# Fused attention: the value matmuls of both query halves of a key tile issued together, behind the third score pair of the next tile

## The chip, the cores and the metric

One core of a Trainium2 chip runs the whole program in one launch. The metric is device time in microseconds (us), as the median of several executions. All stretches, rows and traces below are from one profiled execution of that core. Its engines are TensorE (PE, with its weight loads shown apart as PEld), VectorE (DVE), ScalarE (ACT), GpSimd (POOL) and the queue of SyncE (SP), which issues DMAs.

## The reference, cut to what matters

The program is two adaLN blocks over `x` of 4 batches x 1024 tokens x 128 channels. Each block is attention and then a mixture of experts. The change lies in the attention of the second block, which has a dense part of 16 heads of width 8 and a sparse part over the same tokens, here for one batch of `s` = 1024 tokens:

```
scores = einsum('bhqd,bhkd->bhqk', q, k) / sqrt(8)      # dense, 16 heads
ctx = einsum('bhqk,bhkd->bhqd', softmax(scores), v)
QK = einsum('bqr,bkr->bqk', Q, K) / 8                   # sparse, one head
topv, topi = top_k(softmax(QK), 204)                    # kept and normalised
sparse_output = sparse_attn @ V
fused = sigmoid(lam) * (ctx @ Wo + bo) + (1 - sigmoid(lam)) * sparse_output
```

(The line of `QK` divides by the root of 64; two more matmuls, a layer norm and a feed-forward follow.)

## The kernel before, in words

`attend` (L1693) runs that attention. It takes 4 batches x 4 groups of 4 heads, and the dense part of a group in 8 key tiles of 128 keys. A group is 32 steps, `for n in range(STEPS)`; step n is one head (`n % 4`) of one key tile (`n // 4`). Below, "score n" is the score pair of step n, "tile k" is scores 4k to 4k+3, and j is `n % 4`.

- **TensorE, score (L1931).** `score(b, group, n)` computes 128 keys x 1024 queries of one head in two bf16 matmuls of 512 columns into `scores_ps[n % 2]`, one of two PSUM buffers. So it waits (through `after`, L1690) until the exponential of score n - 2 is done.
- **ScalarE, exponential (L1911).** One activation of 128x1024 reads `scores_ps[n % 2]` and writes `probs[:, kt % 2, j, :]`. At j = 0 it also waits until the value matmuls of the tile before the last have read that half of `probs`.
- **TensorE, values (L1948).** `values(b, group, kt, c)` multiplies the probabilities of all four heads of tile kt with `v_pad` for one half c of the queries. These are four fp32 matmuls with 32 output columns each, in four column tiles of the array, and each is recorded as two (8 records). They accumulate over the tiles into `pv_ps`. They need all four exponentials of their tile. Those of tile kt are issued in tile kt + 1; those of the last tile of a group stand in tile 0 of the next group.
- **TensorE, side work.** `PE_AT` = (0, 4, 8, 11, 15, 19, 23) places seven pieces behind the scores (and behind values) of those steps, in one shared PSUM tile `misc`: the sparse scores of two row tiles (L1966) at 0 and 4, the turn of the dense result (L1973) at 8, the turn of the sparse weights (L1980) at 11 and 19, and the sparse values (L1987) at 15 and 23.
- **ScalarE, side work.** Six pieces at `ACT_AT`: the row excess (L1875) behind exponentials 3 and 8, the sparse exponential (L1884) behind 14 and 22, the copy of turned weights (L1888) behind 12 and 20.
- **VectorE.** It works through a fixed list a group: a search for the threshold of the top 204 of each row (L2099, six rounds), the weighing of the last group's rows (L2109 to L2134), the copy of the finished `pv_ps` (L2037), the copies of the sparse scores (L2041), and the output of heads and rows. The copy L2037 waits for the value matmuls of tile 7, c = 1, which TensorE issues behind score 2 of the next group. From that copy it goes on to weigh the second row tile and then to copy sparse scores 1 (L2041, L2043); the turn of the dense result at step 8 (L1973) waits for that.

Everything is ordered by hand: each engine runs its list in order, and semaphores tie the lists together (`exp_done`, `scored`, `pv_done`, `misc_made`, `misc_used`). SP's loads for a later group and POOL's staging of `v_pad` (L1863) wait on the same semaphores.

Of the kernel before, what the change touches and what calls it, by code (L numbers as in the profile page):

```python
# [16 lines left out]
NT = T // P  # L17
# [1669 lines left out]
def after(eng, sem, count):  # L1687

    if not isinstance(count, int) or count > 0:
        eng.wait_ge(sem, count)  # L1690


def attend(nc, g, f, scratch):  # L1693
# [10 lines left out]
    with ExitStack() as ctx:  # L1704
# [63 lines left out]
        def use(b, group, k):  # L1768

            if k < 2:  # L1770
                return b * (USES * GROUPS) + (USES * group - 4 + k) if not (group == 0 and isinstance(b, int)) else k + 1
            return b * (USES * GROUPS) + (USES * group + 3 + k)

        def last_use(k):

            return USES * (B * GROUPS - 1) + 1 + k

        def before(b, group):

            return (b, group - 1) if group > 0 else (b - 1, LAST)  # L1780

        def over_batches(eng, body, end):

            body(0, True)
            with eng.Fori(1, B) as b:
                body(b, False)
            end(B - 1)

        with nc.Block() as block:
# [131 lines left out]
            @block.tensor  # L1921
            def _(pe):

                def score(b, group, n):
                    kt, j = n // 4, n % 4
                    if n == 0:
                        pe.wait_ge(packs_loaded[group % 2], 16 * LOADS * (b * 2 + group // 2 + 1))

                    after(pe, exp_done, b * PER + group * STEPS + n - 1)
                    for c in range(2):  # L1930
                        ins = pe.matmul(  # L1931
                            scores_ps[n % 2][:, c * 512 : c * 512 + 512],
                            k_pack[:, group % 2, j, kt * P : kt * P + P],
                            q_pack[:, group % 2, j, c * 512 : c * 512 + 512],
                            start=True,
                            stop=True,
                        )
                    ins.then_inc(scored, 1)

                def values(b, group, kt, c):  # L1940
                    if c == 0:
                        pe.wait_ge(exp_done, b * PER + group * STEPS + kt * 4 + 4)
                        if kt == 0:
                            pe.wait_ge(v_staged, b * GROUPS + group + 1)

                            after(pe, pv_kept, b * GROUPS + group)
                    for j in range(4):
                        ins = pe.matmul(  # L1948
                            pv_ps[32 * j : 32 * j + 32, c, :],
                            v_pad[:, group % 2, kt, j, :],  # L1950
                            probs[:, kt % 2, j, c * 512 : c * 512 + 512],
                            start=(kt == 0),
                            stop=(kt == NT - 1),
                        )
                    if c == 1:
                        ins.then_inc(pv_done, 1)

                def free(number):

                    after(pe, misc_used, number - 1)  # L1960

                def sparse_scores(b, group, t):
                    free(use(b, group, t))
                    pe.wait_ge(sq_loaded[t], 16 * (b * GROUPS + group + 1))
                    for c in range(2):
                        ins = pe.matmul(misc[:, c * 512 : c * 512 + 512], sq[:, t, :], f.sparse_k[:, bass.ds(b * T + c * 512, 512)], start=True, stop=True)  # L1966
                    ins.then_inc(misc_made, 1)

                def turn_out(b, group, number):
                    free(number)  # L1970
                    pe.wait_ge(pv_kept, b * GROUPS + group + 1)
                    for n in range(NT):
                        ins = pe.transpose(misc[:, n * P : n * P + P], pv[:, n * P : n * P + P], g.ident[:])  # L1973
                    ins.then_inc(misc_made, 1)

                def turn_weights(b, group, t, number):
                    free(number)
                    pe.wait_ge(w_ready, b * GROUPS + group + 1)
                    for n in range(NT):
                        ins = pe.transpose(misc[:, n * P : n * P + P], e[:, t, n * P : n * P + P], g.ident[:])  # L1980
                    ins.then_inc(misc_made, 1)

                def sparse_values(b, group, t):

                    pe.wait_ge(w_t_ready, (b * GROUPS + group) * 2 + t + 1)
                    for n in range(NT):
                        ins = pe.matmul(  # L1987
                            misc[:, 0:C],
                            w_t[:, n, :],
                            f.sparse_v[:, bass.ds(b * NT + n, 1), :].rearrange("p n c -> p (n c)"),  # L1990
                            start=(n == 0),
                            stop=(n == NT - 1),
                        )
                    ins.then_inc(misc_made, 1)

                def body(b, first):
                    for group in range(GROUPS):
                        prev = before(b, group)
                        alone = first and group == 0
                        side = {PE_AT[0]: lambda: sparse_scores(b, group, 0), PE_AT[1]: lambda: sparse_scores(b, group, 1)}  # L2000
                        if not alone:
                            side |= {
                                PE_AT[2]: lambda: turn_out(*prev, use(*prev, 2)),
                                PE_AT[3]: lambda: turn_weights(*prev, 0, use(*prev, 3)),
                                PE_AT[4]: lambda: sparse_values(*prev, 0),
                                PE_AT[5]: lambda: turn_weights(*prev, 1, use(*prev, 5)),
                                PE_AT[6]: lambda: sparse_values(*prev, 1),
                            }
                        for n in range(STEPS):
                            score(b, group, n)  # L2010

                            if n % 4 in (1, 2):
                                if n >= 4:
                                    values(b, group, n // 4 - 1, n % 4 - 1)
                                elif not alone:
                                    values(*prev, NT - 1, n % 4 - 1)
                            if n in side:
                                side[n]()

                def end(b):  # L2020
                    values(b, LAST, NT - 1, 0)
                    values(b, LAST, NT - 1, 1)
                    turn_out(b, LAST, last_use(2))
                    for t in range(2):
                        turn_weights(b, LAST, t, last_use(3 + 2 * t))
                        sparse_values(b, LAST, t)

                pe.wait_ge(const_ready, 6)
                pe.sem_inc(scored, 1)
                over_batches(pe, body, end)  # L2030

            @block.vector
# [739 lines left out]
```

## Time and profile before

| | us |
|---|---|
| median of 3 executions | 1875.88 |
| the three | 1872.52, 1876.0, 1875.88 |
| span of the profiled execution, first to last instruction | 1874.1 |
| the loop of `attend`, first score to last value matmul | 747 to 1457 |
| one group of 32 steps inside it | 43.9 |

The span counts from the first to the last recorded instruction. Busy shares in the profile's page are means over stages that have different limits, so the loop of `attend` is read by itself, from the views that give instructions in order of time. In those, equal instructions that follow each other are merged into one line. A score pair is two matmul records, a value half eight, and where two score pairs follow each other a line of four stands. The profile models the end of a matmul; its start is recorded.

### The profile page before, as it was taken

What the parts mean: (1) busy time and instruction counts of PE and PEld (TensorE: products, weight loads), DVE (VectorE), ACT (ScalarE), POOL (GpSimd) and SP (SyncE); (2) the same over time, 40 slices, a digit from 0 to 9 for tenths busy, and PEclk for the clock granted to TensorE, in tenths of its full rate; (3) what the DMA queues carried; (4) which work ended last, traced back from release to release, by engine and by line L of the source; (5) the groups of instructions that cost most, each with busy time, mean ns of one, the idle gap of its engine ahead of it and who ended that gap; (6) DMA issues with size and microseconds to landing.
All of it is one profiled execution on the core that took longest, in us unless ns stands there. A gap on an engine that the chain in (4) does not pass through costs nothing. (4 is left out here: it accounts for less than half of the span.)

```text
span 1874.1 us, 27775 instructions
## 1 busy us (share of the span) xinstructions
PE 1327.1 (71%) x8391; PEld 777.8 (42%) x8392; DVE 1205.2 (64%) x3130; ACT 890.4 (48%) x1180; POOL 340.9 (18%) x368
## 2 busy tenths in 40 slices
PE   4577742899905650899999999999999487246830
PEld 3355532899903420233333333333333355235830
DVE  2655563466666660688888878888888477642442
ACT  2333310334403430888888878888888133012200
POOL 0000012763340003000000000000000023217664
PEclk9888965899957785999999999999999788557975
DMA  6700000343311232222222112121220110202322
GB/s 190 219 0 0 0 12 18 104 115 90 90 34 62 83 107 36 31 36 37 34 35 31 31 32 32 32 31 33 31 32 4 40 53 1 90 13 90 104 70 74
DMA packets 118806, 101.01 MB, mean 54 GB/s; under 512 B 10466, under 2 KB 96192, under 8 KB 118656
## 3 DMA queue, kind: packets, MB, share of 16 engines
q1 hardware_dynamic: 107264, 81.42, 18.9%
q0 software_dynamic: 8192, 16.79, 3.2%
q10 hardware_dynamic: 3248, 1.56, 0.3%
q8 instruction: 49, 0.80, 0.2%
q14 instruction: 53, 0.43, 0.1%
HBM read 56.35 MB, written 43.38 MB: 53 GB/s over the span
## 5 line engine op out<-in xcount | busy, mean ns | idle before, releaser
L1911 ACT ACTIVATE probs<-scores_ps 128x1024 f32<-128x1024 f32 x512 | 508.4, 1026 | 147.5 <-PE scores_ps L1931 144.4
L1931 PE MATMUL scores_ps<-q_pack,k_pack 128*128 128x512 bf16 x1024 | 293.3, 383 | 75.2 <-DMA q_pack<-shift_pieces_dram 48.8
L1948 PE MATMUL pv_ps<-probs,v_pad 128*32 128x512 f32 x2048 | 272.8, 605 | 1.1 <-ACT probs L1911 1.1
L2099 DVE TENSOR_SCALAR_CACHE_REDUCE junk<-sparse_scores,at 128x1024 f32<-128x1024 f32 x192 | 245.6, 1279 | 6.9
L1931 PEld LDWEIGHTS scores_ps<-q_pack,k_pack 128*128 128x128 bf16 x1024 | 72.8, 97 | 363.5 <-ACT probs L1911 168.1
L941 POOL DMA_INDIRECT picked_experts<-expert_rows_dram,pick x128 | 132.9, 1039 | 112.9 <-SPq L1041 44.3
L603 POOL DMA_INDIRECT expert_rows_dram<-expert_input,send x128 | 123.2, 962 | 146.8 <-issue 86.6
L1863 POOL COPY v_pad<-v 128x256 f32 x16 | 6.2, 400 | 639.5 <-PE pv_ps L1948 639.3
L1105 ACT ACTIVATE hidden_experts<-pre_experts 128x512 f32<-128x512 f32 x94 | 59.3, 631 | 107.0 <-DVE pre_experts L1064 66.4
L1127 PE MATMUL up_ps_experts<-x_t_experts,up_weights_now_experts 128*128 128x128 f32 x752 | 104.0, 283 | 0.8 <-ACT x_t_experts L1098 0.7
L1064 DVE TENSOR_TENSOR pre_experts<-up_ps_experts,weights_t 128x512 f32<-128x512 f32 x94 | 64.6, 687 | 57.0 <-PE up_ps_experts L1127 56.9
L1134 PE MATMUL down_ps_experts<-weights_t,hidden_experts 128*128 x736 | 97.2, 275 | 0.0
L1127 PEld LDWEIGHTS up_ps_experts<-x_t_experts,up_weights_now_experts 128*128 128x128 f32 x752 | 93.4, 196 | 2.9 <-ACT x_t_experts L1098 1.1
L1134 PEld LDWEIGHTS down_ps_experts<-weights_t,hidden_experts 128*128 128x128 f32 x736 | 89.5, 192 | 0.0
L1948 PEld LDWEIGHTS pv_ps<-probs,v_pad 128*32 128x32 f32 x2048 | 40.4, 108 | 110.4 <-issue 108.4
L549 PE MATMUL ctx_ps<-probs_t,v 128*128 128x128 f32 x288 | 45.3, 308 | 41.9 <-DVE probs_t L425 36.1
L2041 DVE TENSOR_SCALAR_CACHE_REDUCE sparse_scores<-misc_ps 128x1024 f32<-128x1024 f32 x32 | 39.2, 1225 | 50.5 <-PE misc_ps L1966 48.5
L1987 PEld LDWEIGHTS misc_ps<-sparse_v,sparse_w_t 128*128 128x128 f32 x512 | 63.7, 196 | 7.2 <-ACT sparse_w_t L1888 2.9
L1987 PE MATMUL misc_ps<-sparse_v,sparse_w_t 128*128 (+1 forms) x512 | 64.3, 280 | 2.2 <-ACT sparse_w_t L1888 2.2
L332 POOL TENSOR_TENSOR ln_rstd<-ln_var_eps,minus_half 128x8 f32<-128x8 f32 x8 | 13.2, 1649 | 280.8 <-DVE ln_var_eps L304 280.8
L1223 DVE TENSOR_SCALAR hidden_experts<-up_ps_experts,weights_t 128x160 f32<-128x160 f32 x64 | 21.5, 379 | 66.4 <-PE up_ps_experts L1269 57.2
L1966 PE MATMUL misc_ps<-sparse_k,sparse_q_tile 128*128 (+1 forms) x128 | 62.9, 615 | 0.0
(329 smaller groups left out, 2302.2 us busy)
## 6 DMA issues: line engine op xcount, KB each, us to landing
q_pack<-q_pieces_dram SPq DMA_DIRECT2D x144, 64.0 KB
k_pack<-k_pieces_dram SPq DMA_DIRECT2D x144, 64.0 KB
expert_rows_dram<-zeros SPq DMA_DIRECT2D x1, 6400.0 KB, 21.3
x_rows_experts<-expert_rows_dram SPq DMA_DIRECT2D x25, 256.0 KB
expert_rows_dram<-y_rows_experts SPq DMA_DIRECT2D x46, 128.0 KB
expert_rows_dram<-zeros SPq DMA_DIRECT2D x1, 3584.0 KB, 31.2
x_rows_experts<-expert_rows_dram SPq DMA_DIRECT2D x5, 640.0 KB, 4.6
q_pieces_dram<-q_pieces SPq DMA_DIRECT2D x12, 256.0 KB, 2.4
```

Of the source, the lines that this page charges most:

```text
L603: pool.indirect_dma_start(self.rows, bass.IndirectOffsetOnAxis(ap=self.send[:, k, n : n + 1], axis=0), self.h[:, n, :], None).then_inc(sen ...
L941: pool.indirect_dma_start(self.y[:, b, k, n, :], None, moe.rows, bass.IndirectOffsetOnAxis(ap=moe.pick[:, b, k, n : n + 1], axis=0)).then_ ...
L1064: dve.tensor_tensor(pre[:, k % 2], up_ps[k % 2][:], up_bias(e).unsqueeze(2).to_broadcast([P, FC, P]), ALU.add).then_inc(pre_ready, 1)
L1105: act.activation(hidden[:, k % 2], pre[:, k % 2], ACT.Gelu).then_inc(hidden_ready, 1)
L1127: ins = pe.matmul(up_ps[k % 2][:, c, :], up_now[:, k % UNROLL, c, :], x_t[:, k % UNROLL, :], start=True, stop=True)
L1134: ins = pe.matmul(down_ps[k % 2][:, 0:C], hidden[:, k % 2, c, :], down_w(e, c), start=(c == 0), stop=(c == FC - 1))
L1911: act.activation(probs[:, kt % 2, j, :], scores_ps[n % 2][:], ACT.Exp, scale=SCALE1).then_inc(exp_done, 1)
L1931: ins = pe.matmul(scores_ps[n % 2][:, c * 512 : c * 512 + 512], k_pack[:, group % 2, j, kt * P : kt * P + P], q_pack[:, group % 2, j, c * ...
L1948: ins = pe.matmul(pv_ps[32 * j : 32 * j + 32, c, :], v_pad[:, group % 2, kt, j, :], probs[:, kt % 2, j, c * 512 : c * 512 + 512], start=(k ...
L1966: ins = pe.matmul(misc[:, c * 512 : c * 512 + 512], sq[:, t, :], f.sparse_k[:, bass.ds(b * T + c * 512, 512)], start=True, stop=True)
L1987: ins = pe.matmul(misc[:, 0:C], w_t[:, n, :], f.sparse_v[:, bass.ds(b * NT + n, 1), :].rearrange("p n c -> p (n c)"), start=(n == 0), stop ...
L2099: step(dve.tensor_scalar(junk[:], s[:, t, :], at[:, t : t + 1], None, ALU.is_ge, ALU.add, accum_out=count[:, t : t + 1]))
```

## The change

Before, the half c = 0 of the value matmuls is issued behind score 1 of a tile (j = 1) and the half c = 1 behind score 2 (j = 2). Now both are issued behind score 2. Which tile they belong to, what they wait for and what they signal stay the same, and so do all other lists.

```diff
@@ attend, TensorE, body @@
                         for n in range(STEPS):
                             score(b, group, n)
 
-                            if n % 4 in (1, 2):
-                                if n >= 4:
-                                    values(b, group, n // 4 - 1, n % 4 - 1)
-                                elif not alone:
-                                    values(*prev, NT - 1, n % 4 - 1)
+                            if n % 4 == 2:
+                                for c in range(2):
+                                    if n >= 4:
+                                        values(b, group, n // 4 - 1, c)
+                                    elif not alone:
+                                        values(*prev, NT - 1, c)
                             if n in side:
                                 side[n]()
```

## Rows read from the trace of the kernel before

**Rows 1.** The page, busy time and tenths by 40 slices of the span

```profile
PE 1327.1 (71%) x8391; PEld 777.8 (42%) x8392; DVE 1205.2 (64%) x3130; ACT 890.4 (48%) x1180; POOL 340.9 (18%) x368
PE   4577742899905650899999999999999487246830
```

**Rows 2.** Windows: length, busy time and count of each engine, granted clock, DMA share

```profile
core 0: us, PE busy (x) PEld busy (x) DVE busy (x) ACT busy (x) POOL busy (x), PEclk, DMA share, GB/s
...
791.00:1450.00 659.00, 626.28 (x3815) 222.96 (x3813) 564.48 (x1492) 557.41 (x626) 5.43 (x14) 1.00 0.22 31
```

**Rows 3.** Waits of 791 to 1450 us: us in total, times, longest

```profile
PEld scores_ps L1931 <- ACT probs L1911: 149.1, 195, 1.2
```

**Rows 4.** Timeline of TensorE, a tile without side work (start us, us, engine)

```profile
1046.94 1.04 PE L1931 MATMUL scores_ps<-q_pack,k_pack 128*128 128x512 bf16 x4
1048.66 0.60 PE L1931 MATMUL scores_ps<-q_pack,k_pack 128*128 128x512 bf16 x2 [0.69 <-ACT probs L1911]
1049.20 1.06 PE L1948 MATMUL pv_ps<-probs,v_pad 128*32 128x512 f32 x8
1050.19 0.60 PE L1931 MATMUL scores_ps<-q_pack,k_pack 128*128 128x512 bf16 x2
1050.73 1.06 PE L1948 MATMUL pv_ps<-probs,v_pad 128*32 128x512 f32 x8
1051.73 1.04 PE L1931 MATMUL scores_ps<-q_pack,k_pack 128*128 128x512 bf16 x4
```

**Rows 5.** Timeline of ScalarE, the same tile

```profile
1046.05 1.02 ACT L1911 ACTIVATE probs<-scores_ps 128x1024 f32<-128x1024 f32 x1 [0.25 <-PE scores_ps L1931]
1047.58 2.85 ACT L1911 ACTIVATE probs<-scores_ps 128x1024 f32<-128x1024 f32 x3 [0.51 <-PE scores_ps L1931]
```

**Rows 6.** Timeline behind the loop: both halves of the last tile's value matmuls

```profile
1455.21 1.92 PE L1948 MATMUL pv_ps<-probs,v_pad 128*32 128x512 f32 x16 [1.11 <-ACT probs L1911]
```

**Rows 7.** Timeline of TensorE, one group: third scores of its tiles and the side work

```profile
1008.73 1.88 PE L1966 MATMUL misc_ps<-sparse_k,sparse_q_tile 128*128 x4
1010.45 0.59 PE L1931 MATMUL scores_ps<-q_pack,k_pack 128*128 128x512 bf16 x2
...
1013.51 1.04 PE L1931 MATMUL scores_ps<-q_pack,k_pack 128*128 128x512 bf16 x4
...
1021.05 1.09 PE L1973 MATMUL misc_ps<-ident,pv 128*128 128x128 f32 x8 [0.86 <-DVEq L2043]
1021.98 0.59 PE L1931 MATMUL scores_ps<-q_pack,k_pack 128*128 128x512 bf16 x2
...
1025.03 0.60 PE L1931 MATMUL scores_ps<-q_pack,k_pack 128*128 128x512 bf16 x2
...
1026.35 1.03 PE L1931 MATMUL scores_ps<-q_pack,k_pack 128*128 128x512 bf16 x4
...
1029.97 0.60 PE L1931 MATMUL scores_ps<-q_pack,k_pack 128*128 128x512 bf16 x2
...
1032.20 1.33 PE L1931 MATMUL scores_ps<-q_pack,k_pack 128*128 128x512 bf16 x4
...
1035.99 0.60 PE L1931 MATMUL scores_ps<-q_pack,k_pack 128*128 128x512 bf16 x2
```

**Rows 8.** Timeline of ScalarE in that group, side work and what follows

```profile
1015.07 1.14 ACT L1875 ACTIVATE above_mean<-sparse_scores,minus_mean 128x1024 bf16<-128x1024 f32 x1
...
1016.20 3.08 ACT L1911 ACTIVATE probs<-scores_ps 128x1024 f32<-128x1024 f32 x3
...
1027.06 1.02 ACT L1911 ACTIVATE probs<-scores_ps 128x1024 f32<-128x1024 f32 x1 [0.36 <-PE scores_ps L1931]
```

**Rows 9.** Timeline of VectorE, the copy that waits for the value matmuls

```profile
1013.64 1.23 DVE L2037 COPY pv<-pv_ps 128x1024 f32<-128x1024 f32 x1 [1.45 <-PE pv_ps L1948]
```

**Rows 10.** Timeline of TensorE, the first group: one operation at either clock

```profile
748.25 3.62 PE L1966 MATMUL misc_ps<-sparse_k,sparse_q_tile 128*128 128x512 f32 x4
...
754.77 1.88 PE L1966 MATMUL misc_ps<-sparse_k,sparse_q_tile 128*128 128x512 f32 x4
```

## The prediction

> **What bounds the kernel now.** I read the page first. TensorE is the busiest engine (1327.1 of 1874.1 us), and in its tenths the full slices stand together in the middle third [rows 1]. That is the loop of `attend`, 710 us, and only that loop is touched. In its main window of 659 us TensorE is busy 626, VectorE 564, ScalarE 557, all at granted clock 1.00 [rows 2]. So TensorE looks like the limit, with others close behind. The waits say something more exact: its score matmuls waited for ScalarE's exponentials 195 times, 149.1 us in all [rows 3]. An engine that waits 149 us for a partner is not a plain bottleneck. TensorE and ScalarE sit in a loop, and its length is what counts.
>
> Then the timelines. Times are starts unless I say otherwise. Take the tile without side work [rows 4, 5]: the line at 1046.94 is score 3 and the next score 0 (1.04 us for four matmuls against 0.60 for two, so a pair adds 0.44). The next score 1 starts only at 1048.66. What released it? Score 3 started 1046.94, its exponential 1047.58 (0.64 later) and lasts 1.02, and 0.05 after that comes 1048.66. Then score 1 to values 0.54, values to score 2 at 1050.19, values again, and score 3 at 1051.73. The chain is score 1, values, score 2, values, score 3, exponential 3, score 1: 0.54 + 0.99 + 0.54 + 1.00 + 0.64 + 1.02 + 0.05 = 4.78, the 4.79 from 1046.94 to 1051.73. TensorE's own work in a tile is 4 pairs and two value halves, 3.07 + 2 x 0.44 = 3.95 us; 0.84 is waiting. The two PSUM buffers set this: a score may run at most two ahead of the exponentials.
>
> In the whole group [rows 7] score 3 starts at 1007.86 (the side work at 1008.73 less two pairs), 1013.51, ..., 1025.03, 1029.97, 1035.99. The tiles with scores 12 to 15 and 20 to 23 take 4.94 each, those with 16 to 19 and 24 to 27 take 6.02 (two of each kind, the shown rows being the first of each), the plain one 4.79, and tile 0 takes 5.65. From score 3 to score 11 it is 11.52. Sum 5.65 + 11.52 + 2 x 4.94 + 2 x 6.02 + 4.79 = 43.88, one group.
>
> **The change: what it removes.** No instruction goes or comes; no DMA, no load on SP and no wait moves past another, since the half c = 1, which carries the signal `pv_done`, stays behind score 2. What changes is the switching between full-width scores and four-column value matmuls. Two pairs in a row cost 0.44 each, a pair ahead of values 0.54: a switch costs 0.10 [rows 4]. Both halves in a row are seen once, behind the loop: 16 records in 1.92 us [rows 6] where one half shows 1.06, so the second adds 0.86. A following score starts 0.07 ahead of the modelled end (1049.20 + 1.06 against 1050.19), so both halves take 1.85 to the next score in place of 0.99 + 1.00. TensorE saves 0.10 + 0.14 = 0.24 us a tile. With 127 tiles in the loop that is 30 us, if TensorE's own work were the limit.
>
> The Trainium skill, TensorEngine Tiling (Array Packing), section Key Properties, has the rule behind this: changing the tiling mode drains TensorE. The 0.10 and 0.14 agree with it [rows 4, 6]. By that rule alone the sum would be the 30 us of gain; that case is rival 1.
>
> **What it adds.** Scores and exponentials now meet in another rhythm. From score 2 to score 3 it is 0.54 + 1.85 = 2.39 us. In that stretch ScalarE can only work off scores 1 and 2, two exponentials, as the buffers hold no more. Then score 3 lands, ScalarE takes 0.64 + exponential 3, and the next score 2 needs the exponential of the next score 0, which queues behind it. Two exponentials in a row start 0.92 apart (2.85 for three less 1.02, halved [rows 5]). Before, one exponential stood in the loop; after, two. Tile by tile, from score 3 to score 3:
>
> - Plain tile: 0.64 + 0.92 + 1.02 + 0.05 + 2.39 = 5.02, before 4.79: +0.23.
> - Tile 1 and 2 together: the turn of the dense result at step 8 waits for VectorE (0.86 idle, released by DVE [rows 7]), whose list restarts with the copy that waits for the value matmuls, at 1013.64 [rows 9]. This is 0.13 behind score 3 before and will be after, since the last half still ends right ahead of score 3. Its work up to 1021.05 takes 7.54 from score 3. Then 0.93 to score 9, 0.44 to score 10, 2.39 to score 11: 11.30, before 11.52: -0.22. The other path gets to this turn earlier: tile 1 needs 0.64 + 0.90 + 1.13 (the row excess behind exponential 3, 1015.07 to 1016.20 [rows 8]) + 1.02 + 0.05 + 2.39 = 6.13, and two pairs make 7.01 under 7.54.
> - Tiles 3 and 5: score and turn take 1.32 to score 12 (1025.03 to 1026.35 [rows 7]), its exponential starts 0.71 later (1027.06 [rows 8]), then 1.02 + 0.05 to score 14, then 2.39: 5.49, before 4.94: +0.55 each.
> - Tiles 4 and 6: score and sparse values take 2.23 (1029.97 to 1032.20), then again 0.71 + 1.07 + 2.39: 6.40, before 6.02: +0.38 each.
> - Tile 0: TensorE's own list, 0.44 + 0.44 + 1.72 (1008.73 to 1010.45) + 0.44 + 2.39 = 5.43, before 5.65: -0.22.
>
> Sum of a group: 0.23 - 0.22 + 1.10 + 0.76 - 0.22 = +1.65, so 45.5 us in place of 43.9. Fifteen groups give 24.8. The first group has no earlier one, so no values in tile 0 and little side work: I take +0.23 for four tiles, about +1. Together +25.7 us. VectorE has about 1.6 us more slack a group then, and it hides nothing that I count.
>
> The trace holds no tile with both halves in a row inside the loop, so I bound that cost. Lower end: 1.85, from [rows 6]. Upper end: two separate halves, 1.99. I take 1.85, since it is the same instructions in the same order. At the upper end seven stretches of 2.39 a group (tiles 0, 2 to 7) grow by 0.14: 16 more us, +41. Below, if ScalarE's starts came 0.1 earlier in the five tiles 3 to 7, it would be -8: +18.
>
> **The sum.** The profiled execution's span is 1874.1 us; the runs lie at 1872.52 to 1876.0, and their median, 1875.88, is 1.8 above the span. 1874.1 + 25.7 = 1899.8, and on the median 1875.9 + 25.7 = 1901.6 us.
>
> **The rivals.**
> 1. TensorE's own work is the limit, and the 0.24 us a tile comes through: faster, 1875.9 - 30 = 1846 us. For it: 626 of 659 us busy [rows 2]. Against it: the plain tile has 0.84 us of TensorE waiting [rows 4]. It decides once TensorE's 3.71 a tile exceeds the exponential loop. That is so where a tile has over 5.02 - 3.71 = 1.31 us of side work ahead of its score 2, as tile 0 has; elsewhere the step of an exponential would have to fall from 0.92 to below 0.69 to get under the old 4.79. Chance 8%.
> 2. Gains and losses cancel, within 0.2%. Tiles 3 to 7 would have to lose 0.44 us a group in place of the 2.09 that I count, as if the fourth exponential did not stand ahead of score 2. About 1877 us. Chance 5%.
> 3. Both halves in a row inside the loop save nothing: +41, so 1917 us. Against it [rows 6]. Chance 7%.
> 4. The clock. TensorE would wait 1.31 in place of 0.84 us a plain tile. The granted clock was 1.00 in this loop [rows 2], and at its start the same operation took 3.62 us and 6 us later 1.88 [rows 10], half speed (1.2 GHz) and full (2.4 GHz). At half speed the 2.39 of a tile would be about 4.5. If one tile in ten ran so, 13 x 2.1 = 27 us more: about 1929 us. Chance 3%. The Trainium skill, TensorE: Matmul & The Clock Gate, section A second HAM failure mode: psum-queue depth-cycling, tells of short idle stretches between matmul groups making the clock swing; this loop already idles 0.84 us a tile at 1.00, so the trace does not bear that out so far.
> 5. It does nothing: not possible in order, as TensorE runs its list as written; it is in rival 2.
>
> **How the numbers follow.** The forecast has 77%, and by itself lies at 1894 (the +18) to 1908 us. A measurement can tell about 0.2%, 3.8 us, from no change. Slower holds the forecast, rivals 3 and 4: 0.87. Same 0.05, faster 0.08. The range for 8 in 10 reaches to rival 3 above, and below some way under the low bound toward rival 2: 1889 to 1917. It leaves out rival 1, most of 2 and 4.
>
> **What would show it.** In the trace after: 16 value records in one line of about 1.92 us; 2.39 from score 2 to score 3; plain tile 5.02 with score 2, not score 1, waiting for ScalarE; the fourth exponential of a tile behind a gap of over 1.2 us of ScalarE idling; group 45.5; VectorE waiting longer ahead of the copy of sparse scores 0. The forecast is wrong if score 2 starts right behind score 1 in tiles 3 to 7, or if the group is under 43.9.

## The result and the profile after

| | before | after |
|---|---|---|
| median, us | 1874.39 (4 runs) | 1900.6 (4 runs, 1899.05 to 1900.89) |
| ratio, 95% interval | | 1.0135 (1.012 to 1.0149) |
| span of the profiled execution | 1874.1 | 1898.9 |
| first to last start of an exponential L1911 in the loop | 705.65 | 730.32 |
| one group of 32 steps | 43.86 | 45.53 |

The change costs 24.8 us of span, and 24.7 of them lie in the loop of `attend`. A group is measured here and below between starts of the exponential of score 3 in successive groups, in the looped batches, away from the ends of the loop's body (those are 1.5 to 4.5 us longer in every kernel).

The main window of the loop after, to be held against the second line of [rows 2]:

```profile
core 0: us, PE busy (x) PEld busy (x) DVE busy (x) ACT busy (x) POOL busy (x), PEclk, DMA share, GB/s
791.00:1473.00 682.00, 596.59 (x3748) 240.03 (x3813) 565.35 (x1493) 547.95 (x627) 5.43 (x14) 1.00 0.21 30
```

The clock stayed at 1.00. TensorE's busy time fell from 626 to 597 us while the window grew by 23 (67 matmul records are missing from this trace, so the fall is somewhat less). So the engine that was busiest got less to do and the kernel got slower. The waits say where it went. Before (791 to 1450 us), beside [rows 3]:

```profile
ACT probs L1911 <- PE scores_ps L1931: 98.5, 210, 2.6
DVE pv L2037 <- PE pv_ps L1948: 22.2, 15, 2.2
DVE sparse_scores L2041 <- PE misc_ps L1966: 19.9, 15, 2.1
...
PE scores_ps L1931 <- ACT probs L1911: 9.6, 14, 0.7
```

And after (790 to 1475 us):

```profile
PEld scores_ps L1931 <- ACT probs L1911: 237.6, 270, 2.5
ACT probs L1911 <- PE scores_ps L1931: 134.9, 164, 2.4
...
PE scores_ps L1931 <- ACT probs L1911: 72.4, 107, 2.0
DVE sparse_scores L2042 <- PE misc_ps L1966: 45.8, 15, 3.5
DVE pv L2038 <- PE pv_ps L1948: 18.1, 15, 1.5
```

The lines of PE are the ones to read: its score matmuls stood still for exponentials 107 times, 72.4 us in all, in place of 14 times and 9.6 us. That fits the busy time: TensorE was idle 33 of 659 us before and 85 of 682 after. The lines of PEld are of the weight loads, 237.6 us in place of the 149.1 of [rows 3]; most of that time lies beside matmuls that run, so it is no time that TensorE lost. VectorE waits longer for the sparse scores (45.8 in place of 19.9 us) and a little less for the values. The plain tile on TensorE, which answers to [rows 4]:

```profile
1010.88 1.04 PE L1931 MATMUL scores_ps<-q_pack,k_pack 128*128 128x512 bf16 x4
1012.60 0.60 PE L1931 MATMUL scores_ps<-q_pack,k_pack 128*128 128x512 bf16 x2 [0.68 <-ACT probs L1911]
1013.51 0.61 PE L1931 MATMUL scores_ps<-q_pack,k_pack 128*128 128x512 bf16 x2 [0.31 <-ACT probs L1911]
1014.05 1.93 PE L1948 MATMUL pv_ps<-probs,v_pad 128*32 128x512 f32 x16
```

And on ScalarE, beside [rows 5]:

```profile
1011.52 3.77 ACT L1911 ACTIVATE probs<-scores_ps 128x1024 f32<-128x1024 f32 x4 [1.26 <-PE scores_ps L1931]
1016.55 1.94 ACT L1911 ACTIVATE probs<-scores_ps 128x1024 f32<-128x1024 f32 x2 [1.26 <-PE scores_ps L1931]
```

Both halves stand in one line of 16 records. Ahead of them two scores wait, not one: score 1 for exponential 3, and score 2 (1013.51) for the exponential of score 0, which ran behind it. ScalarE then works off four exponentials in a row (3.77) and idles 1.26 until score 3 comes through behind the values. From 1011.52 to 1016.55 it is 5.03 us; before, a plain tile took 4.79 [rows 4].

Tiles 1 and 2 meet VectorE in between. The copy that restarts its list and the turn that waits for it, beside [rows 7, 9]:

```profile
1021.31 1.04 PE L1931 MATMUL scores_ps<-q_pack,k_pack 128*128 128x512 bf16 x4
...
1032.59 0.60 PE L1931 MATMUL scores_ps<-q_pack,k_pack 128*128 128x512 bf16 x2
```

```profile
1021.45 1.23 DVE L2038 COPY pv<-pv_ps 128x1024 f32<-128x1024 f32 x1 [1.21 <-PE pv_ps L1948]
...
1028.85 1.09 PE L1973 MATMUL misc_ps<-ident,pv 128*128 128x128 f32 x8 [0.35 <-DVEq L2044]
```

The copy starts 0.14 behind score 3 (1021.31), the turn 7.54 behind it. Score 11 follows at 1032.59, 11.28 behind score 3.

### The profile page after: what moved, and what is told of

The parts are those of the page before. It is cut to its first block and busy times, and to the rows that moved or that the text cites. A ratio compares the mean times of both kernels' runs of the same rounds, so it can differ in the third digit from the quotient of the medians.

```text
span 1898.9 us, 27703 instructions
## 1 busy us (share of the span) xinstructions
PE 1301.7 (69%) x8319; PEld 800.6 (42%) x8392; DVE 1205.7 (63%) x3130; ACT 881.1 (46%) x1180; POOL 340.6 (18%) x368
## 3 DMA queue, kind: packets, MB, share of 16 engines
HBM read 56.35 MB, written 43.38 MB: 53 GB/s over the span
## 5 line engine op out<-in xcount | busy, mean ns | idle before, releaser
L1911 ACT ACTIVATE probs<-scores_ps 128x1024 f32<-128x1024 f32 x512 | 498.6, 1027 | 180.6 <-PE scores_ps L1931 179.7
L1931 PE MATMUL scores_ps<-q_pack,k_pack 128*128 128x512 bf16 x952 | 267.5, 383 | 137.0 <-ACT probs L1911 79.5
L1948 PE MATMUL pv_ps<-probs,v_pad 128*32 128x512 f32 x2048 | 246.2, 598 | 1.1 <-ACT probs L1911 1.1
L1931 PEld LDWEIGHTS scores_ps<-q_pack,k_pack 128*128 128x128 bf16 x1024 | 77.7, 98 | 354.7 <-ACT probs L1911 259.1
L1948 PEld LDWEIGHTS pv_ps<-probs,v_pad 128*32 128x32 f32 x2048 | 53.4, 109 | 132.1 <-issue 130.5
L1064 DVE TENSOR_TENSOR pre_experts<-up_ps_experts,weights_t 128x512 f32<-128x512 f32 x94 | 64.6, 687 | 56.8 <-PE up_ps_experts L1127 56.6
```

What stands on the lines that cost most here:

```text
L1064: dve.tensor_tensor(pre[:, k % 2], up_ps[k % 2][:], up_bias(e).unsqueeze(2).to_broadcast([P, FC, P]), ALU.add).then_inc(pre_ready, 1)
L1911: act.activation(probs[:, kt % 2, j, :], scores_ps[n % 2][:], ACT.Exp, scale=SCALE1).then_inc(exp_done, 1)
L1931: ins = pe.matmul(scores_ps[n % 2][:, c * 512 : c * 512 + 512], k_pack[:, group % 2, j, kt * P : kt * P + P], q_pack[:, group % 2, j, c * ...
L1948: ins = pe.matmul(pv_ps[32 * j : 32 * j + 32, c, :], v_pad[:, group % 2, kt, j, :], probs[:, kt % 2, j, c * 512 : c * 512 + 512], start=(k ...
```

## The experiments

The theory: two PSUM buffers tie scores and exponentials into a loop, and the change put a second exponential into it. The rivals named a cost in TensorE's own stream, or counted switches alone. The edits below replace the five lines of the change by a table of places, `VALUES_AT[n // 4][c] == n % 4`: behind which score each half is issued, tile by tile (the tables are written short here). Before is (1,2) in all tiles, the changed kernel (2,2).

```diff
+VALUES_AT = ((3, 3),) * 8                                     # behind3
+VALUES_AT = ((2, 2), (1, 2), (2, 2)) + ((1, 2),) * 5          # tiles02
+VALUES_AT = ((1, 2),) * 3 + ((2, 2),) * 5                     # tiles3to7
+VALUES_AT = ((1,1),(1,2),(1,1),(1,2),(1,1),(0,2),(1,3),(1,2)) # placed
+VALUES_AT = ((1, 1),) * 8                                     # behind1
...
                         for n in range(STEPS):
                             score(b, group, n)
 
-                            if n % 4 in (1, 2):
-                                if n >= 4:
-                                    values(b, group, n // 4 - 1, n % 4 - 1)
-                                elif not alone:
-                                    values(*prev, NT - 1, n % 4 - 1)
+                            for c in range(2):
+                                if VALUES_AT[n // 4][c] == n % 4:
+                                    if n >= 4:
+                                        values(b, group, n // 4 - 1, c)
+                                    elif not alone:
+                                        values(*prev, NT - 1, c)
```

**Both halves behind score 3.**

> Both value halves behind score 3 of each tile. Theory (the loop of scores and exponentials through two PSUM buffers sets the pace): TensorE's instructions are those of the changed kernel with the same number of switches, but now nothing is scored ahead while the 1.85 us of values run: score 3, values, score 0, exponentials 0 and then on, so ScalarE idles through most of the values. About 51.4 us a group in place of 43.9 and 45.5, +120 us on before, some 1995 us. Rival (the loss lies in TensorE's own stream: two halves in a row cost more than they save, wherever they stand): as the changed kernel, 45.5 a group, +26 us.

Measured: 2000.08 us, ratio 1.0677 (1.0656 to 1.0698), 51.8 us a group, beside 1995 and 51.4 expected. The same instructions with the same number of switches as in the changed kernel, moved by one score, cost another 100 us. A cost in TensorE's stream can't do that. A tile of it on TensorE:

```profile
1001.72 1.92 PE L1949 MATMUL pv_ps<-probs,v_pad 128*32 128x512 f32 x16
1003.58 0.61 PE L1932 MATMUL scores_ps<-q_pack,k_pack 128*128 128x512 bf16 x2
1004.02 1.88 PE L1967 MATMUL misc_ps<-sparse_k,sparse_q_tile 128*128 x4
1005.74 1.03 PE L1932 MATMUL scores_ps<-q_pack,k_pack 128*128 128x512 bf16 x4
1007.45 0.60 PE L1932 MATMUL scores_ps<-q_pack,k_pack 128*128 128x512 bf16 x2 [0.69 <-ACT probs L1912]
```

**Tiles 0 and 2 alone, and tiles 3 to 7 alone.**

> Both halves behind score 2 in tiles 0 and 2 alone, elsewhere as before. Theory: in these tiles score 2 does not wait for an exponential, so the switch saved comes through, about 0.23 us in each: 43.4 us a group, -7 us, some 1867 us. Rival (a loss of 0.21 us in every tile that has both halves in a row): +7 us.

> Both halves behind score 2 in tiles 3 to 7, tiles 0 to 2 as before. Theory: here the exponential of the next score 0 comes into the loop ahead of score 2, 0.23 to 0.55 us a tile: 46.0 us a group, +33 us on before, so more than the whole change costs. Rival (a loss of 0.21 us in every tile alike): 5 of 8 tiles, +17 us.

Measured: tiles02 1872.66 us, ratio 0.9982 (0.9971 to 0.9993), 43.38 a group; tiles3to7 1907.26 us, ratio 1.0174 (1.0157 to 1.0191), 46.01 a group. Both groups are the forecast ones to 0.02, the parts have opposite signs, and -0.48 and +2.15 add up to the whole change's +1.67. A rival with an equal loss a tile is out. Of tiles02's gain, 6.0 us show in the loop (699.7 against 705.6 from first to last exponential), and 3.4 in the median, where 7 had been expected; a difference of that size outside the loop is within the scatter of the runs.

**Both halves behind score 1.**

> Both halves behind score 1 of each tile. Theory: the same loop one step earlier; the score whose exponential stands ahead of the values is another, and two exponentials are again in the loop: 45.3 us a group, +23 us on before. Rival (the number of switches counts alone): as the changed kernel if it loses by what it issues in a row, +26 us; or -30 us if the halves in a row are good and only score 2 was the wrong place.

Measured: 45.34 a group, as expected, and 5.03 in its plain tile. The time was 2072.73 us, beside 2047.87 for before in the same set of runs, ratio 1.0113 (1.0079 to 1.0146). That set (behind1, the short exponentials, placed2) ran on another chip, and there the kernels took some 170 us more, outside this loop: the stages ahead of it took 855 us in the trace, against 747. So these kernels are read by ratio and by their groups. Score 2 was not a badly chosen place; halves in a row cost at either.

**Short exponentials.** Each covers 256 of 1024 columns. The other probabilities are set to 1 once, ahead of the loop, so these two kernels leave out three quarters of the exponentials.

```diff
-                            act.activation(probs[:, kt % 2, j, :], scores_ps[n % 2][:], ACT.Exp, scale=SCALE1).then_inc(exp_done, 1)
+                            act.activation(probs[:, kt % 2, j, 0:256], scores_ps[n % 2][:, 0:256], ACT.Exp, scale=SCALE1).then_inc(exp_done, 1)
```

> Order of before, but each exponential covers 256 of its 1024 columns (three quarters of the probabilities are a constant, set once): one exponential takes about 0.39 us and they follow each other at 0.28. All matmuls, side work and waits stay. To be read beside short_after. Theory: the loop through ScalarE becomes shorter than TensorE's own list; 42.4 us a group in place of 43.9. Rival (the loss of the changed order lies in TensorE's stream): no statement on this one alone.

> Order of the changed kernel with the same short exponentials. Theory: with the exponential nearly out of the loop the saved switches come through and the sign turns: 41.9 us a group against 42.4 of short_before, some 8 us faster than it. Rival (the loss lies in TensorE's stream or in what waits for the value matmuls): it stays 1.6 us a group slower, 26 us in all.

Measured: 42.35 and 41.92 a group, 2019.03 and 2014.76 us (ratios 0.9875, 0.9847 to 0.9903, and 0.9848, 0.9826 to 0.9869). By the groups the sign turned: -0.43 in place of +1.67. The whole times agree in direction, but their intervals overlap; the statement rests on the traces. The plain tile of short_before, then of short_after, from score 3 to score 3:

```profile
1059.98 1.69 PE L1932 MATMUL scores_ps<-q_pack,k_pack 128*128 128x512 bf16 x6
1061.60 1.06 PE L1949 MATMUL pv_ps<-probs,v_pad 128*32 128x512 f32 x8
1062.60 0.61 PE L1932 MATMUL scores_ps<-q_pack,k_pack 128*128 128x512 bf16 x2
1063.14 1.06 PE L1949 MATMUL pv_ps<-probs,v_pad 128*32 128x512 f32 x8
1064.13 1.04 PE L1932 MATMUL scores_ps<-q_pack,k_pack 128*128 128x512 bf16 x4
```

```profile
1058.01 2.20 PE L1932 MATMUL scores_ps<-q_pack,k_pack 128*128 128x512 bf16 x8
1060.14 1.92 PE L1949 MATMUL pv_ps<-probs,v_pad 128*32 128x512 f32 x16
1061.99 1.04 PE L1932 MATMUL scores_ps<-q_pack,k_pack 128*128 128x512 bf16 x4
```

4.15 us and 3.98: near TensorE's own 3.95 and 3.71, with a rest of the exponential left in. In the first group, where plain tiles follow each other, it is 4.15 and 3.91, the whole 0.24. The group gains only 0.43, as the changed order still takes some 0.06 us more in each of tiles 3 to 6 (4.86 in place of 4.80, 5.77 in place of 5.71). ScalarE's side work keeps its full length there; that this is why was not tried.

**A third score buffer.** These kernels leave out all side work of the loop (the sparse part, the turn of the dense result, VectorE's list but for the copy of `pv_ps`), so that every tile is a plain one. That frees the PSUM tile `misc`. The two with three buffers have, besides the cut work:

```diff
-        scores_ps = [a.ps(f"scores1_ps{i}", [P, T]) for i in range(2)]
+        scores_ps = [a.ps(f"scores1_ps{i}", [P, T]) for i in range(3)]
...
-                    after(pe, exp_done, b * PER + group * STEPS + n - 1)
+                    after(pe, exp_done, b * PER + group * STEPS + n - (2 if group or n > 1 else 1))
```

and both sides take buffer `(group * STEPS + n) % 3`.

> Order of the changed kernel with the sparse part's work left out of the loop on TensorE, ScalarE and VectorE, so that every tile is a plain one; two score buffers. Theory: every tile is the loop 2.39 + 0.64 + 0.92 + 1.02 + 0.05: 5.02 us a tile, 40.2 a group. Rival (the losses come from side work that meets the value matmuls): a plain tile is TensorE's own 3.71, 29.7 a group.

> Order of before, the same work left out, and the PSUM tile that it used now a third score buffer, so that a score waits for the exponential three before it. Theory: the loop is broken and TensorE's own list decides, 3.95 us a tile, 31.6 a group, in place of 4.79 and 38.3 with two buffers. Rival (ScalarE's answer to each score sets the tile however many buffers there are): 38 a group.

> As bare3_before with the order of the changed kernel. Theory: with the loop broken the saved switches come through: 3.71 us a tile on TensorE, ScalarE's four exponentials at 0.91 being 3.65, so 29.7 to 30.5 a group, under bare3_before: the change is a gain of 1 to 2 us a group with three buffers where it is a loss with two. Rival (the order itself costs): over bare3_before by 0.23 a tile, 1.8 a group.

Measured a group: bare2_after 40.23, bare3_before 34.19, bare3_after 32.91 (times 1800.91, 1700.24 and 1683.1 us, two runs each). A tile: 5.03, 4.25, 4.11. No kernel without side work was run in the order of before with two buffers. Its tile stands in the trace of before: 4.79 in [rows 4], and 4.78 to 4.79 in four tiles of the first group. So the change costs 0.24 a tile with two buffers and saves 0.14 with three: its sign hangs on the buffers. The sizes with three buffers were missed, 34.2 for 31.6 and 32.9 for 29.7 to 30.5. I had called the loop broken, and it is not. A tile of bare3_before and one of bare3_after:

```profile
1003.21 1.47 PE L1911 MATMUL scores_ps<-q_pack,k_pack 128*128 128x512 bf16 x6
1004.93 1.06 PE L1928 MATMUL pv_ps<-probs,v_pad 128*32 128x512 f32 x8 [0.25 <-ACT probs L1892]
1005.93 0.60 PE L1911 MATMUL scores_ps<-q_pack,k_pack 128*128 128x512 bf16 x2
1006.46 1.07 PE L1928 MATMUL pv_ps<-probs,v_pad 128*32 128x512 f32 x8
1007.46 1.47 PE L1911 MATMUL scores_ps<-q_pack,k_pack 128*128 128x512 bf16 x5
```

```profile
1003.13 1.47 PE L1911 MATMUL scores_ps<-q_pack,k_pack 128*128 128x512 bf16 x6
1004.85 0.60 PE L1911 MATMUL scores_ps<-q_pack,k_pack 128*128 128x512 bf16 x2 [0.25 <-ACT probs L1892]
1005.38 1.92 PE L1928 MATMUL pv_ps<-probs,v_pad 128*32 128x512 f32 x16
1007.24 1.47 PE L1911 MATMUL scores_ps<-q_pack,k_pack 128*128 128x512 bf16 x6
```

In the first, the wait stands ahead of the value matmuls: they need exponential 3 themselves, a wait on data that no buffer takes away. The loop is score 3, exponential 3 (0.64 + 1.02 + 0.05), values, score 2, values, score 3: 1.71 + 1.00 + 0.53 + 1.00 = 4.24. In the second, score 2 still waits for exponential 3 over its buffer: 1.71 + 2.39 = 4.10. One exponential stands in either loop, and the halves in a row come through as a gain. It is 0.14 and not 0.24: the 0.10 that before pays between score 1 and the first half falls into its wait for exponential 3.

**Places chosen by the chain.**

> Each tile gets the place of its two halves by the chain of that tile: behind scores (1,1) in tile 0, (1,2) in 1, (1,1) in 2, (1,2) in 3, (1,1) in 4, (0,2) in 5, (1,3) in 6, (1,2) in 7. Theory: halves in a row where side work already gave ScalarE a reserve or where score 2 does not wait, halves apart where the loop is tight: 42.4 us a group, -23 us on before, some 1851 us. Rival (only the number of switches counts, a gain of 0.24 us a grouped tile, three of them here): -11 us at most.

> Places of the two halves by tile as (2,2), (1,3), (1,3), (2,2), (1,3), (1,1), (1,3), (1,2), and side work moved a step or so: on TensorE the turn of the dense result behind score 9, the turns of weights behind 12 and 19, the sparse values behind 16 and 23; on ScalarE the row excess behind exponentials 3 and 9, the sparse exponentials behind 15 and 21, the copies of turned weights behind 12 and 19. Theory: 41.1 us a group, -44 us on before, some 1832 us; VectorE's own list of about 41 us a group is then next. Rival (TensorE is as good as full already, 626 of 659 us): no more than the -17 us that the first placement brought.

> The second placement once more, beside fresh runs of before, for its ratio. Its groups took 41.2 us in the loop against 43.9. Theory: -39 us in the loop as there, ratio 0.979. Rival: part of it is given back behind the loop, ratio 0.984 as in the first runs.

Measured: placed 42.44 a group, 1858.72 us, ratio 0.992 (0.9903 to 0.9937); expected were 42.4 and 1851, so its group came as computed. The loop got 19.5 us shorter and not 23, as the first group took 0.5 us more and the second of those at the ends of the loop's body gained nothing; the rival's 11 at most is out all the same. placed2 41.2 a group, 2012.28 us on the other chip, ratio 0.9835 (0.9814 to 0.9856), and once more 0.9801 (0.9785 to 0.9818), 1839.31 us beside 1877.1. Expected were 41.1 and 44 us of gain; it is 36 and 38, as a group gained 2.6 and not 2.8, and the first one 1.6. This kernel is faster than both, 38 us under before; in the loop it is 666.8 us from first to last exponential against 705.6, -39, so nothing is given back behind it. Its edit is the table and the side work:

```diff
-PE_AT = (0, 4, 8, 11, 15, 19, 23)
-ACT_AT = (3, 8, 14, 22, 12, 20)
+PE_AT = (0, 4, 9, 12, 16, 19, 23)
+ACT_AT = (3, 9, 15, 21, 12, 19)
+VALUES_AT = ((2, 2), (1, 3), (1, 3), (2, 2), (1, 3), (1, 1), (1, 3), (1, 2))
```

Its window and waits:

```profile
791.00:1410.00 619.00, 604.87 (x3731) 229.00 (x3799) 560.53 (x1483) 549.23 (x624) 5.43 (x14) 1.00 0.23 33
```

```profile
PEld scores_ps L1932 <- ACT probs L1912: 173.8, 282, 0.8
...
ACT probs L1912 <- PE scores_ps L1932: 56.6, 124, 2.7
```

ScalarE waits 56.6 us for scores in place of 98.5 before. TensorE is busy 605 of 619 us (98%), and the view has no line in which its score matmuls wait for ScalarE: what is left of such waits (PEld, at most 0.8 each) lies beside running matmuls. So TensorE's own list is all but the limit here, as rival 1 had it for the changed kernel. How much of the gain is the table's and how much the side work's was not tried apart.

## Why the prediction was right

- **Forecast 1901.6 us, measured 1900.6.** The step that decides, that the exponential of the next score 0 comes into the loop, is in the trace after (score 2 waits, 1013.51), and the third buffer and the short exponentials show that it is the cause.
- **A misread line.** The prediction took the 149.1 us of [rows 3] for waits of TensorE's matmuls, and from them that TensorE was "not a plain bottleneck". They are the idle time of its weight loads. The matmuls themselves waited 9.6 us for ScalarE, in the plain tiles, so before, TensorE was close to full. The forecast does not rest on that line: its sum comes from the timelines of the tiles, where the 0.69 of the plain tile is read rightly.
- **One sign of it came in part.** Score 2 alone was to wait in the plain tile; there score 1 waits too (0.68, then 0.31). In tiles 3 to 6 score 2 alone waits, as forecast.
- **The unseen operation.** Both halves in a row were priced at 1.85 to the next score, from behind the loop [rows 6]; in the loop the line shows 1.92 to 1.93 of 16 records, as there. Rival 3 is out.
- **Tile by tile**, from score 3 to score 3: plain 5.03 (forecast 5.02), tiles 1 and 2 11.28 (11.30), the group 45.53 (45.5). tiles02 and tiles3to7 hold the negative and positive terms apart.
- **VectorE's chain** of 7.54 us moved with score 3 as forecast. It hides that tile 1 alone got longer: the turn's idle time fell from 0.86 [rows 7] to 0.35.
- **Small terms.** The first group was taken at four times +0.23; it measured +0.3 (41.42 to 41.73). The prediction left out that ScalarE's sparse exponential already stretched two of its tiles to 5.31 before, and they became 5.03. The start ahead of it (+0.45) and the last group (+1.9 behind its exponential 3) made that good. The groups behind the first in the first batch lost 1.52 each and not 1.65, and the two at the ends of the loop's body 1.3 and 1.2. These five lost 1.2 us less than counted, which is the difference between 25.7 and 24.7 to 0.2.
- **Rival 1** (TensorE's own work, 1846 us) fell on the step that it left out: a saving on the busiest engine counts only where it doesn't wait. It is right in the plain tiles of the first group of short_after, where the whole 0.24 a tile came through.
- **Rival 4** did not come: granted clock 1.00 in the window.

## What to carry to other kernels

When two engines hand tiles to each other through two buffers, write down the loop, one lap of scores and exponentials, before counting busy time; a long piece in one engine's list is free only if the other has work in reserve for its whole length. Two buffers hold two exponentials (1.9 us) in reserve at most, and with 1.85 us of values between scores it was 3.04 us from score 2 to the start of exponential 3 (1013.51 to 1016.55), so ScalarE idled. Place such pieces tile by tile where side work already gave the partner a reserve; here that, with some side work moved as well, turned +25 us into -38 with the same instructions. And read waits from the engine's own lines: idle weight loads beside running matmuls are no loss.

## What the runs showed of the hardware that was not expected

A switch between full-width matmuls and those in four column tiles costs 0.10 us into the values (0.54 from a score to them, 0.44 to another score), and the second of two halves in a row saves 0.14 us, in the loop (16 records in 1.92 to 1.93 us) as behind it (1.92, [rows 6]). The time of the same kernel moved by some 170 us between two chips (1877 against 2048 us), while groups inside the loop kept their length: 41.24 us for the second placement on both. From first to last exponential of the loop that kernel took 666.8 and 666.7 us; the stages ahead of it and behind it were longer. Why stays open.
